# A three-layer transformer kernel with a rotation behind it: the set-up by first need, the skew product in it, and own tiles for attention's weights

## The chip, the cores and the metric

The kernel runs on one core of one Trainium2 chip. The metric is the device time of one execution in microseconds, as the median of several runs. The engines are TensorE (PE; its weight loads are PEld), VectorE (DVE), ScalarE (ACT), GpSimd (POOL) and SyncE (SP), which issues nearly all of the DMAs.

## What is computed

`x` is 32 sequences of 128 tokens with 144 channels, `cond` has one row of 144 for each sequence. Three transformer layers, modulated by `cond`, run one after another, and a rotation stands behind them. The first layer, in the reference's words:

```python
ada = jax.nn.silu(c) @ W_ada + b_ada
shift_msa, scale_msa, gate_msa, shift_mlp, scale_mlp, gate_mlp = jnp.split(ada, 6, axis=-1)
h = _modulate(_layernorm(x), shift_msa, scale_msa)
x = x + gate_msa * _attention(h, W_qkv, b_qkv, W_proj, b_proj)
h = _modulate(_layernorm(x), shift_mlp, scale_mlp)
mlp = jax.nn.gelu(h @ W_fc1 + b_fc1, approximate=True) @ W_fc2 + b_fc2
x = x + gate_mlp * mlp
```

Attention has 16 heads of 9 channels. The second layer's MLP is a mixture of four experts, of which each token takes two; the third layer has weights and biases on its layer norms. The last step:

```python
v = jax.nn.silu(cond) @ W.T + b                 # W: 2016 rows
A = A.at[:, iu, ju].set(v).at[:, ju, iu].set(-v)
R = expm(A)                                     # one 64 x 64 rotation for each sequence
U, _ = jnp.linalg.qr(P)                         # P: 144 x 64
z = jnp.einsum('btn,nd->btd', x, U)
z_rot = jnp.einsum('btd,bde->bte', z, R)
x_rot = x + jnp.einsum('btd,nd->btn', z_rot - z, U)
```

Everything is float32.

## The kernel before, in words

**Tiling.** All of x stays on the chip (tile `X`), tokens on partitions. The 144 channels of a contraction, with a row of ones for the bias, are 128 rows and 17 rows, so a weight matrix is loaded as a 128-row part and a 17-row part. The products of h with the weights are made of numbers in fp32r, as split products (`split_product`, L1000): the weights' rounded part (`Whi`), what it leaves (`Wlo`), and a third tile (`W3`) that stacks the 17 rows three times, against h in the same three forms (`hhi`, `hlo`, `h3`). One q/k product is 8 matmuls, shown as `L1000 x8`. The weights for both attention and MLP use the same three tiles, so each layer's weights are split twice on VectorE: `split` (L350 to L363) takes the 128-row part in two instructions and the 17-row part in pieces of 512 columns, through the tile `hshi`, which is h's too.

**Set-up.** SyncE loads, in this order: cond and constants, the layer-norm columns, the weights of the gates (`in_ada_gate`), x in four quarters, the weights of the columns (`in_ada_col`: shift and scale for three layers, twice, with the channels on partitions), the q/k/v weights of layer 0 (`in_wqkv`, 128 rows and three times 17), then the output weights `wp` of attention. TensorE transposes P for the QR decomposition, makes the gates (L978, L979) and then the columns, as 24 pairs of small products with the weights stationary (L989, L990). VectorE takes the statistics of the 32 sequences in a loop (L318) behind a wait for all of x, copies the gates, adds one to the scale columns on their way out of PSUM (L328), applies the third layer's layer-norm weights (L336, L342), splits the q/k/v weights, makes variance and inverse root of all sequences at once (`rstd_all`, L371 to L390), clears the tiles that attention needs clear (L427 to L432), and normalises the first pair (L396, L399). The gates are stored to memory and come back as one row for each sequence (`gate<-gates`, L246).

**Attention.** `pair(i)` for i from -2 to 17 runs two sequences in a pipeline of several stages on all engines: normalise, transpose (L1021), modulate on ScalarE (L809), four q/k products, each with a copy on ScalarE (L825) and a stacking step on VectorE (L446) that frees the one PSUM bank for the next; a v product, scores for the row maximum (L1057), the maximum (L458), scores again transposed (L1064), exponentials on ScalarE (L830), the product with v (L1079), the output product (L1111). pair(-2) and pair(-1) are the beginning of the pipeline only. The MLP runs in 8 groups of 4 sequences. During the last pair VectorE splits the MLP's weights, in the last MLP group the next layer's q/k/v weights (L350 and so on, called from `dense_step`), ahead of that group's last gated sums (L623) and statistics (L646).

**The tail.** Behind the last layer SyncE loads 17 rows of the skew weights (`in_skew_w`, 4096 columns; the 128-row part was loaded during the last layer), TensorE makes the 32 x 4096 skew product in eight banks (L1260, L1261), VectorE and ScalarE copy it out, SyncE stores it (`skew<-BIG`) and loads it back as 64 x 64 matrices (`BIG<-skew`), and the exponential of the matrices follows. The QR decomposition runs on GpSimd, in its own loop, with a broadcast through memory by GpSimd's queue in each step (`QB<-QA`).

The order of each engine's work is the order in which its program is written; engines meet by semaphores. SyncE's queue is one stream: a load behind a wait waits too.

## Time and profile before

| | us |
|---|---|
| median of 3 runs | 1677.52 (1673.40 to 1680.44) |
| profiled execution | 1683.87 |
| its span in the profile | 1682.1 |
| TensorE busy | 1447.5 (86%) |
| TensorE weight loads | 1187.5 (71%) |
| VectorE busy | 1022.9 (61%) |
| GpSimd busy | 830.7 (49%) |
| ScalarE busy | 750.1 (45%) |
| mean granted TensorE clock | 0.891 of full speed |

Busy shares are means over the whole span. The profile also gives, for any stretch of the span, a chain of waits: from its last instruction back to what released it, so that its pieces add up to the time that passed. A timeline lists each engine's instructions in order of time, with the idle time ahead of each in brackets and what ended it. The trace's times start with the span. PSA, PSB and PS are the PSUM tiles, without their numbers; BIG is one large tile that many stages share.

### The profile page before, as it was taken

Reading aid. Unit: us, or ns where it says so; the run is one execution under the profiler, and the core shown is the slowest. Engines: PE = TensorE matmul, PEld = TensorE weight load, DVE = VectorE, ACT = ScalarE, POOL = GpSimd, SP = SyncE. Lnnn points to the kernel's source line nnn. Section 1 sums busy time; section 2 is a strip of 40 time slices with the busy share of each in tenths; the row PEclk is TensorE's granted clock in tenths of the full one; section 3 lists DMA queues with packets and bytes.
Section 4 is the critical chain, followed back from the end, with each engine's and each line's share of the span. In section 5 each row is a group of like instructions: output and inputs, shape, how many; then the busy total and the mean of one; then the engine's idle time right before and its main releaser. Section 6 shows DMA issues by size and latency. Waiting matters only on the chain.

```text
span 1682.1 us, 39613 instructions
## 1 busy us (share of the span) xinstructions
PE 1447.5 (86%) x14380; PEld 1187.5 (71%) x14380; DVE 1022.9 (61%) x2471; ACT 750.1 (45%) x1484; POOL 830.7 (49%) x2444
## 2 busy tenths in 40 slices
PE   5499999679599999679999999679999949775599
PEld 3378888468488888469898999568888739705545
DVE  4589999645579999743333333459999845306511
ACT  0166666366266677343333332147767536300011
POOL 4666666666566566666667777777750000000000
PEclk9999999789689999879999999869999959956755
DMA  5211111312311211211112233333420021100001
GB/s 134 31 10 18 18 17 18 45 12 33 85 18 16 17 16 16 37 13 13 11 12 15 16 17 12 36 12 22 25 18 12 12 64 22 24 16 14 2 15 42
DMA packets 49363, 41.46 MB, mean 25 GB/s; under 512 B 8371, under 2 KB 45542, under 8 KB 48695
## 3 DMA queue, kind: packets, MB, share of 16 engines
q0 software_dynamic: 4224, 7.45, 12.4%
q1 hardware_dynamic: 44971, 31.79, 8.1%
q8 instruction: 104, 1.70, 0.4%
q14 instruction: 64, 0.52, 0.1%
HBM read 28.85 MB, written 2.99 MB: 19 GB/s over the span
## 4 chain that ended last, share of the span: by engine, by line
PE 82%; DVE 10%; ACT 3%; DMA 2%; issue 2%; SPq 1%; DVEq 0%; ACTq 0%
PE PS L1000 17%; PE PS L1211 14%; PE PSA L1000 12%; PE PSA L1057 6%; PE PS L1079 6%; PE PS L1093 3%; PE PS L1101 3%; PE PS L1214 2%; PE PS L1111 2%; DVE BIG L758 2%; PE PS L1112 1%; PE PSA L1269 1%; PE PS L1106 1%; PE PS L1329 1%; PE PS L1311 1%
## 5 line engine op out<-in xcount | busy, mean ns | idle before, releaser
L1211 PE MATMUL PS<-w,BIG 128*128 128x144 f32 (+1 forms) x1920 | 267.4, 287 | 4.7 <-DVE BIG L627 3.4
L1211 PEld LDWEIGHTS PS<-w,BIG 128*128 128x128 f32 (+1 forms) x1920 | 254.4, 191 | 12.8 <-DVE BIG L627 3.6
L909 ACT ACTIVATE BIG<-PSA 128x512 f32<-128x512 f32 (+1 forms) x224 | 131.6, 595 | 267.2 <-PE PSA L1000 267.1
L458 DVE TENSOR_REDUCE BIG<-PSA 128x8 f32<-128x1024 f32 x192 | 234.3, 1221 | 21.2 <-PE PSA L1057 17.2
L830 ACT ACTIVATE BIG<-PSB 128x1024 f32<-128x1024 f32 x192 | 196.8, 1025 | 105.6 <-PE PSB L1064 105.1
L825 ACT ACTIVATE qkhi<-PS 128x512 fp32r<-128x512 f32 x192 | 114.7, 597 | 101.8 <-PE PS L1000 95.1
L1000 PE MATMUL PS<-hhi,Whi 128*128 128x256 f32 x384 | 133.4, 347 | 21.8 <-DVE KK L446 10.1
L1057 PE MATMUL PSA<-KK,Q 32*128 32x128 f32 x1536 | 130.6, 288 | 4.7 <-DVE BIG L458 2.2
L1057 PEld LDWEIGHTS PSA<-KK,Q 32*128 32x128 f32 x1536 | 103.3, 190 | 39.5 <-issue 23.3
L1079 PE MATMUL PS<-BIG 128*32 128x128 f32 x3072 | 126.3, 283 | 4.1 <-ACT BIG L830 3.7
L1064 PE MATMUL PSB<-Q,KK 32*128 32x128 f32 x1536 | 127.9, 284 | 1.9 <-ACT BIG L830 1.9
L627 DVE SCALAR_TENSOR_TENSOR BIG<-PS,BIG 128x144 f32<-128x144 f32 x96 | 35.2, 368 | 151.4 <-PE PS L1214 151.4
L1377 POOL TENSOR_TENSOR qtree<-qtree 128x36 f32<-128x36 f32 (+3 forms) x384 | 101.6, 265 | 30.1
L1000 PE MATMUL PSA<-hhi,Whi 128*128 128x512 f32 (+1 forms) x224 | 102.4, 457 | 14.4 <-ACT BIG L909 8.8
L1000 PE MATMUL PS<-hhi,Wlo 128*128 128x256 f32 x384 | 113.2, 295 | 0.0
L1000 PE MATMUL PS<-hlo,Whi 128*128 128x256 f32 x384 | 112.8, 294 | 0.0
L1000 PE MATMUL PS<-h,W 128*128 128x256 f32 x384 | 112.4, 293 | 0.0
L1395 POOL MEMSET qprod<- 128x2 f32 x63 | 6.5, 103 | 208.6 <-DMA QB<-QA 208.6
L1000 PEld LDWEIGHTS PS<-hhi,Whi 128*128 128x128 f32 x384 | 76.6, 200 | 45.3 <-DVE KK L446 24.5
L1370 POOL DMA_DIRECT2D QB<-QA x128 | 81.9, 640 | 47.4 <-POOL QA L1410 18.9
L1064 PEld LDWEIGHTS PSB<-Q,KK 32*128 32x128 f32 x1536 | 100.9, 185 | 2.9 <-issue 2.5
L1382 POOL TENSOR_TENSOR qtree<-qtree 128x4 f32<-128x4 f32 (+3 forms) x384 | 83.1, 216 | 30.1
(272 smaller groups left out, 3877.1 us busy)
## 6 DMA issues: line engine op xcount, KB each, us to landing
gate<-gates SPq DMA_DIRECT2D x96, 72.0 KB, 2.9
mgate<-gates SPq DMA_DIRECT2D x96, 72.0 KB, 2.8
X<-in_x SPq DMA_DIRECT2D x4, 576.0 KB, 8.5
out<-X SPq DMA_DIRECT2D x8, 288.0 KB, 2.4
BIG<-in_skew_w SPq DMA_DIRECT2D x1, 2048.0 KB
BIG<-in_wqkv SPq DMA_DIRECT2D x3, 584.0 KB
w<-in_w SPq DMA_DIRECT2D x1, 1440.0 KB
BIG<-in_wm SPq DMA_DIRECT2D x1, 1154.0 KB
```

The lines of the kernel that those rows point to most:

```text
L458: V.tensor_reduce(nmax[:, :, 3 * HD + 2 * HP * a:3 * HD + 2 * HP * a + HP + 1:HP].rearrange("p g r -> p r g"), PSA[:, :].rearrange("p (r g ...
L825: S.activation(qkhi[:, :], PS[4][:, :], ACT.Copy).then_inc(qk_hi, 1)
L830: S.activation(PT[:, u % 2, a, :], PSB[:, :], ACT.Exp, scale=float(HD) ** -0.5).then_inc(exp_done, 1)
L909: S.activation(hm[0:rows, slot, :], PS[(par * FTOT[l] + j) % 2][0:rows, :], gelu).then_inc(gelu_done, 1)
L1000: last = mm(o, a, b, start=(k == 0), stop=(k == 3))
L1057: one = mm(PS[r][:, g * 128:(g + 1) * 128], Q[rows, par, g, q0:q0 + 128], KK[rows, par, g, q0:q0 + 128], start=True, stop=True)
L1064: two = mm(PS[2 + r][:, g * 128:(g + 1) * 128], KK[rows, par, g, q0:q0 + 128], Q[rows, par, g, q0:q0 + 128], start=True, stop=True)
L1079: last = mm(PS[6][p0:p0 + HP, at:at + 128], VA[:, u, G * g + 2 * a + r, :], PT[:, u % 2, a, (G * r + g) * 128:(G * r + g + 1) * 128], star ...
L1211: last = mm(o, hm[0:rows, slot, s * 128:(s + 1) * 128], w2[0:rows, FT * e + k, :], start=(k == 0), stop=(l != 1 and k == FT - 1))
L1370: pool.dma_start(QB[k % 2][:, k:C], row).then_inc(q_row[k % 2], 16)
L1377: link(R.tensor_tensor(t[:, 0:n, :], a[:, :, 0:half], a[:, :, half:2 * half], ALU.add))
L1382: link(R.tensor_tensor(t[:, 0:n, :], a[:, :, 0:half], a[:, :, half:2 * half], ALU.add))
```

## The change

In SyncE's program the loads come in another order: column weights of layer 0 by themselves, the first quarter of x, the q/k/v weights, the second quarter, the column weights of layers 1 and 2, the gates' weights, the last two quarters; then, behind the wait for the constants, the skew weights (in two halves of 2048 columns), `wp` and the layer-norm columns. The stores of the gates and of the skew product stand there too, ahead of the loads of the first MLP weights; after the last layer only the load of the matrices is left.

The columns are now products with silu(cond) stationary, 32 columns wide: four kinds of column lie on four strips of 32 in one bank (`column_products`), ScalarE adds one to the scales while it copies the bank, and TensorE transposes them (`columns_turn`). Gates and skew product use four strips in the same manner (`gate_products`, `skew_products`). Layer 0's columns are made first. Those of layers 1 and 2 and the gates are produced behind pair(-2) of layer 0, the skew product behind pair(-1), and `columns_rest` stands behind pair(0).

Statistics, variance and inverse root are functions of a range of sequences: the first 8 sequences are done ahead of pair(-2), the other 24 behind it, their inverse root behind pair(-1). `constant_parts`, the memsets of attention's tiles, stands behind pair(-2) in layer 0.

Attention's weights have tiles `Ahi`, `Alo`, `AW3` for themselves, those of the MLP `Mhi`, `Mlo`, `MW3`. The casts of attention's are ScalarE's (`qkv_cast`), and the 17-row part isn't cut into pieces of 512, for neither. In pair(-2) of layer 0 the q/k products use two banks in turn (`qk_bank`).

```diff
+        Ahi, Alo = sb("Ahi", [C0, WQKV], F32R), sb("Alo", [C0, WQKV], F32R)
+        AW3 = sb("AW3", [128, WQKV], F32R)
+        Mhi, Mlo = sb("Mhi", [C0, WMX], F32R), sb("Mlo", [C0, WMX], F32R)
+        MW3 = sb("MW3", [128, WMX], F32R)
...
+        def qk_bank(pn, j):
+            return PS[6 if pn == 0 and j % 2 else 4]
...
+            def load_ada(l, s):
+                sp.dma_start(AC0[l], d["ada_col"][0:C0, l * AC:(l + 1) * AC]).then_inc(s, 16)
+                sp.dma_start(AC1[l], d["ada_col"][C0:C + 1, l * AC:(l + 1) * AC]).then_inc(s, 16)
+            load_ada(0, ld_ada0)
+            def load_x(q):
                 sp.dma_start(X[:, q * 8 * C:(q + 1) * 8 * C].rearrange("p (b c) -> p b c", b=8),
...
+            load_x(0)
             load_raw("wqkv0", WQKV, ld_wq)
+            load_x(1)
+            load_ada(1, ld_ada)
+            load_ada(2, ld_ada)
+            sp.dma_start(AG0, d["ada_gate"][0:C0, :]).then_inc(ld_gw, 16)
+            sp.dma_start(AG1, d["ada_gate"][C0:C + 1, :]).then_inc(ld_gw, 16)
+            load_x(2)
+            load_x(3)
             sp.wait_ge(s_const, 1)
+            for h in range(2):
+                sp.dma_start(SW0[h], d["skew_w"][0:C0, h * SKH:(h + 1) * SKH]).then_inc(ld_skew, 16)
+                sp.dma_start(SW1[h], d["skew_w"][C0:C + 1, h * SKH:(h + 1) * SKH]).then_inc(ld_skew, 16)
...
+            sp.wait_ge(s_gev, 1)
+            for j in range(4):
+                sp.dma_start(gates_dram[:, j * GT:(j + 1) * GT], gate_rows[j * NB:(j + 1) * NB, :]).then_inc(s_gst, 16)
+            sp.wait_ge(sk_ev, 2)
+            for j in range(4):
+                sp.dma_start(skew_dram[:, j * 1024:(j + 1) * 1024], SV[j * NB:(j + 1) * NB, :]).then_inc(sk_st, 16)
+            sp.wait_ge(s_gst, 64)
+            sp.wait_ge(sk_st, 64)
             for l in range(LAYERS):
-                sp.wait_ge(s_split, SPLITS * (2 * l + 1))
+                sp.wait_ge(a_split, 2 * l + 2)
+                sp.wait_ge(s_cps, LAYERS)
                 load_raw(f"wm{l}", WM[l], ld_wm)
                 wait(sp, f2_done, n_unit(l) * MT)
+                sp.wait_ge(sk_ps, 2)
...
-            sp.dma_start(SW1, d["skew_w"][C0:C + 1, :]).then_inc(ld_skew, 16)
-            sp.wait_ge(sk_ev0, 4)
-            sp.wait_ge(sk_ev1, 4)
-            sp.dma_start(skew_dram, SV).then_inc(sk_st, 16)
-            sp.wait_ge(sk_st, 16)
...
+            def first_stats(q):
+                dve.wait_ge(ld_x[q], 16)
+                for b in range(8 * q, 8 * q + 8):
+                    V.bn_stats(st6[:, b:b + 1, :], xb(b)).then_inc(s_st0, 1)
+            def columns(l, ps):
+                dve.wait_ge(s_ct, 1 if l == 0 else LAYERS)
+                V.tensor_copy(col0[:, l, :, :], ps[:, 0:128].rearrange("p (k n) -> p k n", k=4))
+                V.tensor_copy(col1[:, l, :, :], ps[0:S3, 128:256].rearrange("p (k n) -> p k n", k=4)).then_inc(s_cev, 1)
...
+            def qkv_split(l):
+                wr, wr3 = raw(WQKV)
+                dve.wait_ge(a_cast, 2 * l + 2)
+                V.tensor_tensor(Alo[:, :], wr, Ahi[:, :].bitcast(F32), ALU.subtract).then_inc(a_split, 1)
+                V.scalar_tensor_tensor(AW3[0:S3, :], AW3[0:S3, :].bitcast(F32), K[0:S3, K_MW:K_MW + 1], wr3, ALU.mult, ALU.add)\
+                    .then_inc(a_split, 1)
+            def mlp_split(l):
+                n = WM[l]
+                wr, wr3 = raw(n)
+                dve.wait_ge(ld_wm, 64 * (l + 1))
+                V.tensor_copy(Mhi[:, 0:n], wr)
+                V.tensor_copy(MW3[0:S3, 0:n], wr3).then_inc(m_split, 2)
+                dve.wait_ge(m_split, 4 * l + 2)
+                V.tensor_tensor(Mlo[:, 0:n], wr, Mhi[:, 0:n].bitcast(F32), ALU.subtract)
+                V.scalar_tensor_tensor(MW3[0:S3, 0:n], MW3[0:S3, 0:n].bitcast(F32), K[0:S3, K_MW:K_MW + 1], wr3,
+                                       ALU.mult, ALU.add).then_inc(m_split, 2)
...
+                    first_stats(0)
+                    variance(0, 0, 0, 0, 8)
+                    columns(0, PS[1])
+                    inverse_root(0, 0, 0, 0, 8)
...
+                    if l == 0 and i == -2:
+                        qkv_split(0)
+                        for q in range(1, 4):
+                            first_stats(q)
+                        variance(0, 0, 1, 8, NB)
+                        dve.wait_ge(s_cps, LAYERS)
+                        dve.wait_ge(s_gps, 1)
+                        constant_parts()
+                    if l == 0 and i == -1:
+                        inverse_root(0, 0, 1, 8, NB)
+                    if l == 0 and i == 0:
+                        columns_rest()
...
+            def qkv_cast(l):
+                wr, wr3 = raw(WQKV)
+                act.wait_ge(ld_wq, 64 * (l + 1))
+                S.activation(Ahi[:, :], wr, ACT.Copy).then_inc(a_cast, 1)
+                S.activation(AW3[0:S3, :], wr3, ACT.Copy).then_inc(a_cast, 1)
+            def setup_rest():
+                column_rows(1, PS[2])
+                column_rows(2, PS[0])
+                act.wait_ge(s_gps, 1)
+                S.activation(gate_rows, PS[7][:, 0:GT], ACT.Copy).then_inc(s_gev, 1)
+            def skew_copies():
+                for h in range(2):
+                    act.wait_ge(sk_ps, h + 1)
+                    S.activation(SV[:, h * 512:(h + 1) * 512], PS[6 + h][:, :], ACT.Copy).then_inc(sk_ev, 1)
...
+                    if l == 0 and i == 0:
+                        skew_copies()
...
+                if l + 1 < LAYERS:
+                    qkv_cast(l + 1)
...
+            def column_products(l, ps):
+                for src, s, first in ((AC0, sc0, True), (AC1, sc1, False)):
+                    for kind in range(4):
+                        last = mm(ps[kind * NB:(kind + 1) * NB, 0:XW], s[:, :], src[l][:, kind * XW:(kind + 1) * XW],
+                                  start=first, stop=not first)
+                last.then_inc(s_cps, 1)
+            def columns_turn(l, ps):
+                pe.wait_ge(s_crow, l + 1)
+                nc.tensor.transpose(ps[:, 0:128], crow[:, l, 0:C0], ident)
+                nc.tensor.transpose(ps[0:S3, 128:256], crow[:, l, C0:XW], ident).then_inc(s_ct, 1)
+            def gate_products():
+                pe.wait_ge(ld_gw, 32)
+                for src, s, first in ((AG0, sc0, True), (AG1, sc1, False)):
+                    for j in range(4):
+                        last = mm(PS[7][j * NB:(j + 1) * NB, 0:GT], s[:, :], src[:, j * GT:(j + 1) * GT], start=first, stop=not first)
+                last.then_inc(s_gps, 1)
+            def skew_products():
+                pe.wait_ge(ld_skew, 64)
+                pe.wait_ge(s_gev, 1)
+                pe.wait_ge(qk_lo, 4)
+                for h in range(2):
+                    for src, s, first in ((SW0, sc0, True), (SW1, sc1, False)):
+                        for j in range(4):
+                            at = (j % 2) * 1024 + h * 512
+                            last = mm(PS[6 + h][j * NB:(j + 1) * NB, :], s[:, :], src[j // 2][:, at:at + 512], start=first, stop=not first)
+                    last.then_inc(sk_ps, 1)
+            pe.wait_ge(ld_cond, 48)
+            pe.wait_ge(s_silu, 4)
+            pe.wait_ge(ld_ada0, 32)
+            column_products(0, PS[0])
             pe.wait_ge(q_ld, 64)
             nc.tensor.transpose(PS[6][:, 0:C0], QP[:, 0, :], ident)
             nc.tensor.transpose(PS[6][:, C0:C], QP[0:C - C0, 1, :], ident[0:C - C0, 0:C - C0]).then_inc(q_ps, 1)
...
+            columns_turn(0, PS[1])
...
+                    wait(pe, qk_lo, n - 1 if n < 4 else n)
...
-                pe.wait_ge(va_set, 3 * (l + 1))
                 for i in range(-2, NB // 2 + 2):
+                    if i == 0:
+                        pe.wait_ge(va_set, 3 * (l + 1))
+                    if i == 1:
+                        pe.wait_ge(ld_wp, 160 * (l + 1))
                     pair(i)
...
+                    if l == 0 and i == -2:
+                        pe.wait_ge(ld_ada, 64)
+                        column_products(1, PS[2])
+                        pe.wait_ge(s_crow, 1)
+                        column_products(2, PS[0])
+                        gate_products()
+                    if l == 0 and i == -1:
+                        skew_products()
+                        pe.wait_ge(s_crow, LAYERS)
+                    if l == 0 and i == 0:
+                        pe.wait_ge(sk_ev, 2)
+                        columns_turn(1, PS[7][:, 0:256])
+                        columns_turn(2, PS[7][:, 256:512])
+                        pe.wait_ge(s_cev, LAYERS)
...
-            pe.wait_ge(ld_skew, 32)
-            for c in range(8):
-                mm(PS[c][0:NB, :], sc0[:, :], SW0[:, c * 512:(c + 1) * 512], start=True, stop=False)
-                mm(PS[c][0:NB, :], sc1[:, :], SW1[:, c * 512:(c + 1) * 512], start=False, stop=True).then_inc(sk_ps, 1)
```

SyncE, from the start of its queue, before:

```order
L204 DMA BIG<-in_ada_gate 128x864
L205 DMA BIG<-in_ada_gate 17x864
L207 DMA X<-in_x 128x8x144 x4
L210 DMA BIG<-in_ada_col 128x2148
L211 DMA BIG<-in_ada_col 17x2148
L215 DMA BIG<-in_wqkv 128x1168
L217 DMA BIG<-in_wqkv 17x1168 x3
L223 DMA wp<-in_wp 18x144 [waits constants_set]
```

The same engine after the change, from behind the column weights of layer 0:

```order
L227 DMA X<-in_x 128x8x144
L233 DMA BIG<-in_wqkv 128x1168
L235 DMA BIG<-in_wqkv 17x1168 x3
L227 DMA X<-in_x 128x8x144
L221 DMA BIG<-in_ada_col 128x716
L222 DMA BIG<-in_ada_col 17x716
L221 DMA BIG<-in_ada_col 128x716
L222 DMA BIG<-in_ada_col 17x716
L250 DMA mgate<-in_ada_gate 128x864
L251 DMA BIG<-in_ada_gate 17x864
L227 DMA X<-in_x 128x8x144 x2
L256 DMA BIG<-in_skew_w 128x2048 [waits constants_set]
```

Two of the four x loads and everything of the q/k/v weights are in front of the gates' weights; the last two quarters of x stand behind them, and the skew weights behind these.

VectorE, before, behind the third layer's column steps: the split of the q/k/v weights (the row L363 fills up the semaphore), and the first row of the variance (`mean`):

```order
L350 CAST Whi<-BIG 128x1168 [waits columns_product,constants_set,wqkv_loaded,columns_steps]
L352 TENSOR_TENSOR Wlo<-BIG,Whi 128x1168 [waits weights_split]
L356 CAST hshi<-BIG 51x512
L358 SCALAR_TENSOR_TENSOR W<-hshi,K,BIG 51x512 [waits weights_split]
L356 CAST hshi<-BIG 51x512 [waits weights_split]
L358 SCALAR_TENSOR_TENSOR W<-hshi,K,BIG 51x512 [waits weights_split]
L356 CAST hshi<-BIG 51x144 [waits weights_split]
L358 SCALAR_TENSOR_TENSOR W<-hshi,K,BIG 51x144 [waits weights_split]
L363 MEMSET epst 128x1 [waits weights_split]
L371 TENSOR_TENSOR mean<-st 128x32 [waits first_stats]
```

VectorE after the change, behind the second normalised sequence (the memsets and the step `hlo`, the low part of h, follow these rows):

```order
L384 TENSOR_TENSOR Alo<-BIG,Ahi 128x1168 [waits qkv_weights_cast]
L385 SCALAR_TENSOR_TENSOR AW<-AW,K,BIG 51x1168
L353 BN_STATS st<-X 128x6 [waits x_loaded1]
L353 BN_STATS st<-X 128x6 x7
L353 BN_STATS st<-X 128x6 [waits x_loaded2]
L353 BN_STATS st<-X 128x6 x7
L353 BN_STATS st<-X 128x6 [waits x_loaded3]
L353 BN_STATS st<-X 128x6 x7
L404 TENSOR_TENSOR mean<-st 128x24 [waits first_stats]
L405 TENSOR_TENSOR rtmp<-st 128x24
```

The split waits for casts of ScalarE and not for its own; three waits for quarters of x now lie between the split and `hlo`.

TensorE, before, from the end of the first pair's fourth q/k product through its v product (128x144) to its first scores (`PSA<-KK,Q`):

```order
L1000 MATMUL PS<-h,W 128x256
L1000 MATMUL PS<-Whi,hhi 128x144 [waits hf_ready]
L1000 MATMUL PS<-Wlo,hhi 128x144
L1000 MATMUL PS<-Whi,hlo 128x144
L1000 MATMUL PS<-W,h 128x144
L1000 MATMUL PS<-Whi,hhi 128x144
L1000 MATMUL PS<-Wlo,hhi 128x144
L1000 MATMUL PS<-Whi,hlo 128x144
L1000 MATMUL PS<-W,h 128x144
L1057 MATMUL PSA<-KK,Q 128x128 [waits qk_stacked]
L1057 MATMUL PSA<-KK,Q 128x128 x7
```

TensorE after the change, from the same q/k product to the v product (the scores follow behind it, as before):

```order
L1099 MATMUL PS<-hlo,Ahi 128x256
L1099 MATMUL PS<-h,AW 128x256
L1079 MATMUL PS<-BIG,sc 32x512 [waits qk_stacked,gates_copied,skew_loaded]
L1079 MATMUL PS<-BIG,sc 32x512 x3
L1079 MATMUL PS<-w,sc 32x512 x2
L1079 MATMUL PS<-BIG,sc 32x512 x6
L1079 MATMUL PS<-w,sc 32x512 x2
L1079 MATMUL PS<-BIG,sc 32x512 x2
L1099 MATMUL PS<-Ahi,hhi 128x144 [waits hf_ready,va_set,column_rows_ready]
L1099 MATMUL PS<-Alo,hhi 128x144
L1099 MATMUL PS<-Ahi,hlo 128x144
L1099 MATMUL PS<-AW,h 128x144
```

Sixteen skew matmuls of 32 rows by 512 columns, with three waits ahead of them, now stand between the fourth q/k product and the v product, which itself waits for rows of the other layers' columns.

## Rows read from the trace of the kernel before

**Rows 1.** Chain, the first 120 us: start us, length us, what.

```profile
13.73 11.86 DMA BIG<-in_ada_col
...
67.19 2.09 PE PS L1000 x8
```

**Rows 2.** Timeline of VectorE: start us, us, line, operation, out<-in, count.

```profile
47.61 0.73 DVE L336 SCALAR_TENSOR_TENSOR col<-col,lnc 128x32 f32<-128x32 f32 x4
```

**Rows 3.** Chain over the tail.

```profile
1465.91 12.51 DMA BIG<-in_skew_w
1478.55 1.88 PE PSA L1260 x2
...
1506.24 1.85 PE PS L1261 x2
1508.78 3.86 DMA skew<-BIG
1513.40 4.49 DMA BIG<-skew
1517.91 1.24 DVE BIG L720
```

**Rows 4.** Windows: PE, PEld, DVE, ACT, POOL, PE clock, DMA share, GB/s.

```profile
24.00:25.00 1.00, 0.00 (x0) 0.00 (x0) 0.64 (x3) 0.00 (x0) 0.00 (x0) 1.00 2.20 104
28.00:29.00 1.00, 1.00 (x7) 0.87 (x6) 0.62 (x2) 0.00 (x0) 0.97 (x3) 1.00 0.07 28
36.00:37.00 1.00, 1.00 (x6) 0.87 (x5) 0.00 (x0) 0.00 (x0) 0.67 (x2) 1.00 0.05 13
```

**Rows 5.** DMA issues: tiles, queue, count, KB each.

```profile
BIG<-in_wqkv SPq DMA_DIRECT2D x3, 77.6 KB
...
BIG<-in_skew_w SPq DMA_DIRECT2D x1, 272.0 KB
```

**Rows 6.** Timeline, TensorE and VectorE; brackets: idle before, what ended it.

```profile
10.46 1.62 PE L978 MATMUL PSA<-BIG,sc 128*32 128x432 f32 x2 [2.33 <-DMA BIG<-in_ada_gate]
...
17.80 0.31 DVE L318 BATCH_NORM_STATS2 st<-X  x1 [9.78 <-DMA X<-in_x]
```

**Rows 7.** Timeline of VectorE, before the first product and at a layer's end.

```profile
54.74 0.21 DVE L371 TENSOR_TENSOR mean<-st 128x32 f32<-128x32 f32 x1
...
58.45 0.48 DVE L427 MEMSET BIG<- 128x512 f32 x1 [0.17 <-DVE rstd L390]
...
61.73 0.34 DVE L396 TENSOR_SCALAR xh<-X,mean,rstd 128x128 f32<-128x128 f32 x1
...
438.35 0.93 DVE L646 BATCH_NORM_STATS2 st<-X 128x6 f32<-128x144 f32 x4
```

**Rows 8.** Timeline of TensorE, first scores.

```profile
81.44 1.11 PE L1057 MATMUL PSA<-KK,Q 32*128 32x128 f32 x8
```

**Rows 9.** Timeline of TensorE, a product on four strips.

```profile
315.93 1.08 PE L1079 MATMUL PS<-BIG 128*32 128x128 f32 x16
```

**Rows 10.** Timeline of VectorE, split at the end of layer 0.

```profile
431.33 0.78 DVE L350 CAST Whi<-BIG 128x1168 fp32r<-128x1168 f32 x1
432.14 1.39 DVE L352 TENSOR_TENSOR Wlo<-BIG,Whi 128x1168 fp32r<-128x1168 f32 x1
...
433.90 0.74 DVE L358 SCALAR_TENSOR_TENSOR W<-hshi,K,BIG 51x512 fp32r<-51x512 f32 x1
...
436.19 0.36 DVE L358 SCALAR_TENSOR_TENSOR W<-hshi,K,BIG 51x144 fp32r<-51x144 f32 x1
...
436.68 0.52 DVE L623 TENSOR_TENSOR BIG<-PS,mgate 128x144 f32<-128x144 f32 x2
```

**Rows 11.** Timeline of ScalarE.

```profile
99.69 1.03 ACT L830 ACTIVATE BIG<-PSB 128x1024 f32<-128x1024 f32 x1 [1.33 <-PE PSB L1064]
...
428.30 1.28 ACT L797 ACT_TABLE_LOAD   x1
```

**Rows 12.** Chain in the second pair, from 96 us.

```profile
106.19 1.14 PE PS L1000 x8
```

322 lines of the change are left out of this document (142 added, 180 removed).

## The prediction, made before the changed kernel ran

> **What bounds the kernel now.** I read four views: the chain of work over the first 120 us, the DMA traffic microsecond by microsecond, the timelines at the seams between stages, and the chain over the tail. [rows 1] is the chain of the start: it runs through the landing of the column weights (`in_ada_col`), the column products, the column steps on VectorE (done at 47.6 [rows 2]) and then split, statistics and memsets on VectorE, until the first q/k product starts at 67.19. Nothing of the attention runs before that. At the other end [rows 3] the chain waits 12.5 us for 17 rows of the skew weights, then computes the skew products for 29.5 us (1478.55 to 1508.1), stores them (3.9), loads them back and has the matrices at 1517.91. Between the two, TensorE is nearly always busy, except at five seams, at which VectorE does a weight split that TensorE waits for.
>
> **What a narrow load costs.** [rows 4] decides the start. From 26 to 36 us the DMA share is 0.06 to 0.07, which is one engine of sixteen, at 28 GB/s; at 36 it ends. What is queued last then are three 17-row copies of the q/k/v weights, 77.6 KB each [rows 5]: they run one after another, on one engine. The tail says the same: 272 KB in 17 rows [rows 5] take 12.5 us [rows 3], 26 KB/us behind some 2 us of latency. So I count KB on that one engine: a 128-row load leaves a sixteenth of its size there, a 17-row load all of it. Before: gates 27+57, x 144, columns 67+143, q/k/v 36+233. The landings fit: gates at 10.4, x at 17.8 [rows 6], columns 25.6 [rows 1], q/k/v at 36; that is 18 KB/us from 5 to 17.8, while all engines are busy, and 26 after it, stalls of about 1.2 us by the Householder broadcasts included (the microsecond from 24 in [rows 4]). The Trainium skill ("DMA: Bandwidth & Descriptors", "Why a DMA increments its semaphore by 16 and not by 1") says why: a load runs on the largest number up to 16 that divides its slowest dimension, so 17 rows run on one engine, and always the lowest-numbered. The trace agrees for the three copies; which engine it is, no row shows.
>
> **Part 1: set-up (gain 12.4 us).** The new order on that engine is: columns of layer 0 (22+48 KB), x0 36, q/k/v 269, x1 36, columns of layers 1 and 2 140, gates 84, x2 and x3 72, skew 400. By the rates above: x0 lands at 10, q/k/v at 21.5, x3 at 36.0 (332 KB at 23), the skew weights at 52.4. x3, which was there at 17.8, now comes 18 us later.
> VectorE: the first quarter's statistics, its root and two normalised batches are done by about 17. The split waits for ScalarE's casts, which wait for q/k/v: 21.5 + 2.3 + 2.8 = 26.6. Then it waits for x3 at 36.0, and behind that wait stand the statistics of the last quarter (8 at 0.23 [rows 7] = 1.9), the variance (a third of the 3.7 us from 54.74 to 58.45 [rows 7], 1.2), the memsets (58.45 to 61.8 [rows 7], 3.4) and the low part of h (0.8), which TensorE needs. First q/k product at 36.0 + 7.3 = 43.4 instead of 67.19: 23.8 us earlier. The products of layers 1 and 2 and the gates lie in TensorE's idle time before it.
> From there to the first scores took 14.25 us (67.19 to 81.44 [rows 1, 8]). Now the first four q/k products use two banks, so the next need not wait for copy and stack; at 2.09 us each, with the transposes between, they end after 9.9 us. ScalarE comes with 1.1 us of rows of the other layers ahead of its fourth copy; copy and stack (0.6 + 0.75) bring 55.9. Only then come the skew products (their weights at 52.4 are in time, by 3.5 us), with the v product (1.75) behind them, which before lay beside the stack. The skew products were 29.5 us for 16 matmuls in line [rows 3]; on four strips I take the factor of the one product that runs so: 16 passes of 128 columns in 1.08 us [rows 9] where a quarter of the 0.92 us of a 512-column pass is 0.23, so 3.7 in line, factor 3.5. That is 8.3 us at TensorE's lower level (1.2 GHz). The bounds are 7.4 (factor 4) and 4.2 (the higher level already). The Trainium skill ("TensorEngine Tiling (Array Packing)", "Theoretical Speedup") allows up to 4; by it the sum would be better by 0.9 us. First scores at 55.9 + 8.3 + 1.75 = 65.9, 15.5 us earlier than before.
> Then columns_rest sits between the first and the second pair: four transposes (0.6) and four copies (0.9), then eight small steps (4 in 0.73 [rows 2], so 1.4), all ahead of the max row for which the v product waits: 3.1 us with their waits. 15.5 - 3.1 = **12.4**. The bounds are 0 to 28, see the rivals.
> The stores of gates and skew rows and three loads are now ahead of the first gate row on SyncE. The copies are done at 65, two stores and their wait end near 70, the row lands at about 79 and is first read some 11 us into the second pair, near 95: nothing, by 16 us of cover.
>
> **Part 2: splits (gain 8.2 us).** At the end of a layer the split stood 5.35 us on VectorE (431.33 to 436.68 [rows 10]) ahead of the last two sums. Now the casts are ScalarE's: two of 1168 columns at about 1.15 (1.03 for 1024 [rows 11]), begun when its last gelu is done at 428.3 [rows 11], so ready at 430.6, ahead of VectorE at 431.3. There remain 1.39 and one multiply-add of 1168 columns, 1.43 by the slope from 0.36 (144 columns) to 0.74 (512) [rows 10]: 2.8 + gaps. Gain 2.5, and between layers 1 and 2, where the same stands in a row and ScalarE is idle even longer, 2.7. The three MLP splits lose pieces of 512: each saved piece is about 0.45 us of fixed cost and gaps, one in layers 0 and 2, four in layer 1: 2.7, rounded to 3 with the memset. The bound below is 0, if the out-copies of ScalarE are late instead. Own tiles for attention's weights take no wait away that ended last in any row; I give them nothing.
>
> **Part 3: the tail (gain 46.7 us).** The load, products, copies and store all go. From 1465.91, when the last statistics end, only the load back is left: 1512.66 to 1517.91 was 5.25 us, so the matrices are there at 1471.2 instead of 1517.9. 46.7, bounds 45 and 48: a load begun after a stretch of idle engines is priced by 3.9 to 5.3 in [rows 3]. TensorE is at its lower level both when it starts these matrices now and when it started them before, so I add nothing for it.
>
> **Sum.** 12.4 + 8.2 + 46.7 = 67.3. The profiled execution took 1683.9 and would give 1616.6; the median of the runs is 1677.5, so the forecast is **1610.2 us** (0.960 of before).
>
> **Rivals.**
> *A: the narrow loads are not in the way*, because other engines take them in turn and all ends by bytes. The Trainium skill's fit ("DMA: Bandwidth & Descriptors", "Anatomy of one DMA — SWDGE (gpsimd) path"), 2.0 us and 436 KB per microsecond, is of this kind. By rows: x3 would land as in [rows 6] after some 5 MB, at about 20; then the split and 24 statistics bound VectorE and the first product starts near 31. 12.4 us better than forecast: 1598. Against it stands [rows 4]. 15%.
> *B: the engine runs at 18 KB/us all the way*, as from 5 to 17.8. All through the skew weights 1,117 KB then land at 67, x3 at 44; TensorE waits in front of the skew products with all of attention behind it. 11 us worse: 1621. For it: more of the set-up now goes through with all engines busy, and a queue that is full holds SyncE back. 12%.
> *C: the strips stand in line* and the skew products take 29.5: 21 us worse, 1631. [rows 9] speaks against it. 4%.
> *D: slower than before.* One mechanism: TensorE stays at its lower level into layer 0's attention, since the thin skew products (the 29.5 us of them in [rows 3] never brought it up) and the wait after the first pair come where it used to rise. A q/k product costs 2.09 instead of 1.14 us [rows 1, 12]; a pair of batches, near 14 us at the higher level and full of TensorE work, then costs some 11 more. The 67 us are eaten after 6 pairs of 16; at 10 the kernel takes 1720. Before, the level rises within some 30 us of the first product. 2%.
>
> **How the numbers follow.** The forecast has 67%. The range takes in A and B and the bounds of the tail and splits, 1594 to 1625; outside lie C, D and the ends of the bounds. 0.5% is about what a measurement of this kernel can tell from no change; faster needs less than 1669, which all but D and accidents give: 0.96, same 0.02, slower 0.02.
>
> **What would show it.** First q/k product at 43 (31 for A, 52 for B), with VectorE's longest wait before it on x's last quarter; one engine's share of DMA through 50 us; skew products 8 us, not waiting for their weights; about 3 us of TensorE idle after the first pair; split rows of 2.8 us at both layer seams; the matrices 5.3 us behind the last statistics. I am wrong if the first product comes later than 52, or the skew weights do.

## The result, and the profile after

The changed kernel takes **1605.55 us** (median of 4 runs, 1603.45 to 1612.98) where the kernel before took 1676.84 in the same series: ratio 0.9553, 95% interval 0.9524 to 0.9582. A second series gave 0.9571 (0.9542 to 0.9601). Two executions of the kernel before, at 3418.6 and 7202.8 us in the series of `one_bank`, are slow ones and left out everywhere. The forecast was 1610.2, ratio 0.960. The profiled execution took 1603.45 us, its span is 1601.7, against 1683.87 and 1682.1 before.

The head of the page and its clock row (tenths of full speed, 40 slices):

```profile
PE 1395.5 (87%) x14346; PEld 1162.1 (73%) x14346; DVE 1005.9 (63%) x2430; ACT 756.5 (47%) x1493; POOL 825.9 (52%) x2444
...
PEclk9799999889789999869999999979999997986755
```

The chain of waits over the first 110 us of the changed kernel (start us, length us, what), the lines that answer to [rows 1, 8]:

```profile
9.53 8.04 SPq L222
...
20.47 13.25 DMA X<-in_x
33.74 3.46 DVE st L353 x16
...
42.56 3.79 PE PS L1099 x16
...
52.55 0.76 DVE Q L490
53.31 0.14 issue
53.45 7.52 PE PS L1079 x32
60.97 1.91 PE PS L1099 x8
62.88 1.04 PE PSA L1156 x6
```

The chain no longer runs through the column products, it runs through x, and the first q/k product starts at 42.56 instead of 67.19. Ahead of x it runs through SyncE: the issue of one 17-row load of column weights (L222) took 8.04 us, so that the last quarters of x were issued only at 20.47. At 53.45 stand the skew products. Windows of 2 us of the same kernel (the columns as in [rows 4]) show what x waits for:

```profile
14.00:16.00 2.00, 0.91 (x4) 0.69 (x4) 1.04 (x4) 0.00 (x0) 0.00 (x0) 1.00 0.08 30
16.00:18.00 2.00, 0.21 (x1) 0.00 (x0) 0.00 (x0) 0.00 (x0) 1.58 (x4) 1.00 0.06 26
26.00:28.00 2.00, 0.00 (x0) 0.00 (x0) 1.44 (x7) 0.00 (x0) 1.45 (x3) 1.00 0.06 25
```

A DMA share of 0.06 to 0.08 at 25 to 30 GB/s: one engine of sixteen, as in [rows 4], first during the 17-row copies of the q/k/v weights and again during the narrow part of the columns. VectorE's timeline says the same (the bracket: idle time before, and what ended it); its last three rows are the split at the end of layer 0 and the sums behind it, which answers to [rows 10]:

```profile
23.03 1.38 DVE L384 TENSOR_TENSOR Alo<-BIG,Ahi 128x1168 fp32r<-128x1168 f32 x1 [7.99 <-ACT AW L859]
24.32 1.43 DVE L385 SCALAR_TENSOR_TENSOR AW<-AW,K,BIG 51x1168 fp32r<-51x1168 f32 x1
...
33.74 3.45 DVE L353 BATCH_NORM_STATS2 st<-X 128x6 f32<-128x144 f32 x16 [6.30 <-DMA X<-in_x]
...
413.53 1.36 DVE L384 TENSOR_TENSOR Alo<-BIG,Ahi 128x1168 fp32r<-128x1168 f32 x1
414.81 1.60 DVE L385 SCALAR_TENSOR_TENSOR AW<-AW,K,BIG 51x1168 fp32r<-51x1168 f32 x1
416.34 0.51 DVE L675 TENSOR_TENSOR BIG<-PS,mgate 128x144 f32<-128x144 f32 x2
```

And the chain over the tail, which answers to [rows 3]: the load of the matrices follows the last statistics at once.

```profile
1431.08 0.94 DVE st L698 x4
1432.77 4.42 DMA BIG<-skew
1437.30 1.24 DVE BIG L769
```

Both kernels were profiled a second time (in `before_again` and `after_again`, below). The places where each stage starts or ends, in us from the span's start, read from the timelines (a stage's end is the first row of the next variance). The profile shows a granted clock of 1.00 until its first record of it, also from 42.6 to 46 us of the changed kernel, where matmuls of 256 columns take 0.41 us as at the lower level. So a first rise is read here from the record and from the lengths of matmuls, and the mean clock of a kernel that rises late is shown too high:

| | before | again | after | again | after less before, first pair |
|---|---|---|---|---|---|
| first q/k product | 67.2 | 66.6 | 42.6 | 42.7 | -24.6 |
| first scores | 81.4 | 80.8 | 62.8 | 62.9 | -18.6 |
| TensorE's granted clock first rises | 94.1 | 99.3 | 46.3 | 46.5 | |
| attention of layer 0 ends | 327.9 | 329.7 | 308.1 | 308.1 | -19.8 |
| MLP of layer 0 ends | 439.4 | 441.4 | 418.8 | 418.8 | -20.6 |
| attention of layer 1 ends | 714.9 | 713.9 | 693.8 | 697.0 | -21.1 |
| MLP of layer 1 ends | 1086.9 | 1087.1 | 1061.5 | 1064.5 | -25.4 |
| attention of layer 2 ends | 1357.4 | 1352.9 | 1323.6 | 1333.7 | -33.8 |
| last statistics done | 1465.9 | 1461.2 | 1432.0 | 1442.3 | -33.9 |
| matrices there | 1517.9 | 1513.5 | 1437.3 | 1447.5 | -80.6 |

### The profile page after: what moved, and what is told of

Read it like the earlier page. It is cut to its first block, busy times and chain, and to the rows that moved or that the text cites. A ratio compares the mean times of both kernels' runs of the same rounds, so it can differ in the third digit from the quotient of the medians.

```text
span 1601.7 us, 39391 instructions
## 1 busy us (share of the span) xinstructions
PE 1395.5 (87%) x14346; PEld 1162.1 (73%) x14346; DVE 1005.9 (63%) x2430; ACT 756.5 (47%) x1493; POOL 825.9 (52%) x2444
## 4 chain that ended last, share of the span: by engine, by line
PE 83%; DVE 9%; ACT 3%; issue 3%; SPq 1%; DMA 1%; ACTq 0%; DVEq 0%
PE PS L1099 17%; PE PS L1326 14%; PE PSA L1099 13%; PE PSA L1156 7%; PE PS L1178 7%; PE PS L1192 3%; PE PS L1200 3%; PE PS L1329 2%; PE PS L1210 2%; PE PS L1211 2%; DVE BIG L807 1%; PE PS L1205 1%; PE PSA L1379 1%; PE PS L1437 1%; PE PS L1419 1%
## 5 line engine op out<-in xcount | busy, mean ns | idle before, releaser
L1099 PE MATMUL PS<-hhi,Ahi 128*128 128x256 f32 x384 | 131.5, 343 | 23.8 <-DVE h L441 14.7
L1099 PE MATMUL PSA<-hhi,Mhi 128*128 128x512 f32 (+1 forms) x224 | 102.4, 457 | 14.7 <-ACT BIG L992 9.1
L1099 PE MATMUL PS<-h,AW 128*128 128x256 f32 x384 | 112.2, 292 | 0.0
L1099 PE MATMUL PS<-hlo,Ahi 128*128 128x256 f32 x384 | 111.2, 290 | 0.0
L1099 PE MATMUL PS<-hhi,Alo 128*128 128x256 f32 x384 | 111.2, 290 | 0.0
L1099 PEld LDWEIGHTS PS<-hhi,Ahi 128*128 128x128 f32 x384 | 75.8, 197 | 46.3 <-DVE KK L490 21.0
L1178 PEld LDWEIGHTS PS<-BIG 128*32 128x32 f32 x3072 | 73.2, 110 | 34.5 <-issue 22.9
## 6 DMA issues: line engine op xcount, KB each, us to landing
X<-in_x SPq DMA_DIRECT2D x4, 576.0 KB, 13.8
```

The lines of the kernel that those rows point to most:

```text
L1099: last = mm(o, a, b, start=(k == 0), stop=(k == 3))
L1178: last = mm(PS[6][p0:p0 + HP, at:at + 128], VA[:, u, G * g + 2 * a + r, :], PT[:, u % 2, a, (G * r + g) * 128:(G * r + g + 1) * 128], star ...
```

## The experiments

All ratios are to the kernel before, run on the same chip in the same series.

**The same kernels again.** Nothing is edited.

> The changed kernel itself once more, as the base for the others of this series. My theory of the 80 us between the two profiled executions is 73 us of changed work and some 7 us of which the profiled execution of before was itself longer than its median, so the ratio to before stays at 0.955 (0.952 to 0.958). The rival, that the gain ahead of the tail (33.9 us where I had forecast 20.6) is all the change's, wants 0.951 or less.

Measured: 1611.7 us against 1681.0, ratio 0.9571 (0.9542 to 0.9601). No boundary up to 418.8 differs by more than 0.1 us from the first profiled execution, then layer 1's attention takes 278.2 us instead of 275.0 and layer 2's 269.2 instead of 262.1. The runs of this one kernel lie at 1602.6 with a mean granted clock of 0.905 and at 1616.2 with 0.894; over all runs of the study a line with one slope for all kernels gives 8.5 us (standard error 0.5) for 0.01 of mean clock.

> The kernel before, once more, for a second profiled execution of it. Attention of layer 2 with its seam to the MLP took 8.4 us more in the first profiled execution of before than in that of the changed kernel, where the prediction has 0.5. If that is the granted clock of one execution, the stretch from the first q/k product of layer 2 (1099.1) to its first MLP product (1374.7), 275.6 us, differs by 3 us or more this time, and the time at the boundaries of layer 0 stays within 1 us. If it is the change's, it is 275 to 276 again.

Measured: ratio 0.9991 (0.9963 to 1.0018). From the first q/k product of layer 2 to its first MLP product the execution took 271.0 us (1099.2 to 1370.2), 4.5 less than the first one; layer 0's boundaries differ by 2, more than I had said. So of the 8.4 us that layer 2's attention seems to gain (270.5 to 262.1 in the table), 4.7 go when one execution of before is put for the other, and 7.1 when one of after is. Over this stage the four executions had a granted clock of 0.91 (270.5 us, before), 0.92 (269.2, after again), 0.94 (265.8, before again) and 0.96 (262.1, after): the time goes by the clock and not by the kernel.

**Narrow loads.** Each 17-row load of the set-up in two:

```diff
+            def narrow(dst, src, s):
+                sp.dma_start(dst[0:16, :], src[0:16, :]).then_inc(s, 16)
+                sp.dma_start(dst[16:17, :], src[16:17, :]).then_inc(s, 16)
```

> One thing is changed: each 17-row load of the set-up is issued as 16 rows and 1 row. If a 17-row load runs on one engine and x's third and fourth quarter stood behind 332 KB on it, they land near 17 instead of 33.7, the statistics of three quarters and the memsets follow the split in a row, and the first q/k product starts at 29 (28 to 32) instead of 42.6: 11 to 13 us faster than the changed kernel. If all engines share the bytes anyway (rival A of the prediction), the first product stays at 42 to 43 and the time at that of the changed kernel, or 1 to 2 us above it for the nine further loads that SyncE issues.

Measured: 1598.5 us, ratio 0.9509 (0.9485 to 0.9533), by the medians 13.2 us less than `after_again` in the same series, by the two ratios 10.4, and 12.8 (standard error 1.2) at equal clock. Its chain:

```profile
11.52 9.45 DMA X<-in_x
20.99 3.46 DVE st L360 x16
...
29.78 3.79 PE PS L1106 x16
```

The first q/k product starts at 29.8 instead of 42.6. Same bytes, the same order, no other edit: the place behind narrow loads was the price. SyncE isn't held at a narrow load any more either (none takes over 0.7 us to issue), and it issues the last quarters of x at 11.52. The profiled execution doesn't show all of the gain at once: first scores come 13.8 us earlier (49.0), but attention of layer 0 ends 5.4 us earlier (302.7), with a granted clock of 0.92 over that stretch where the changed kernel had 0.97.

**VectorE's work moved behind.** Statistics, variance and memsets for the later sequences go from behind pair(-2) to behind pair(-1):

```diff
                     if l == 0 and i == -2:
                         qkv_split(0)
+                    if l == 0 and i == -1:
+                        dve.wait_ge(s_cps, LAYERS)
+                        dve.wait_ge(s_gps, 1)
+                        constant_parts()
                         for q in range(1, 4):
                             first_stats(q)
                         variance(0, 0, 1, 8, NB)
```

> The loads stay as in the changed kernel. VectorE's statistics of the last 24 sequences, their variance and attention's memsets are moved from between the split and the low part of h to behind pair(-1) of layer 0, where VectorE is idle for the 7.5 us of the skew products; ScalarE's root for them goes behind its copies of columns and gates. If x's late landing was what held the first q/k product, the next limit is TensorE's own program, where the gates' weights land at about 32 and the gate products end at 34: first q/k product at 34 to 35, 8 us earlier, and the moved work costs 1 to 2 us later, so 6 to 7 us faster than the changed kernel. If the late quarters were not the limit, nothing is gained (0 to 1).

> Both edits of the two runs before together. q/k/v weights land near 10, ScalarE's casts are done at 15.1, the split at 18, and columns and gates lie beside it: first q/k product at 19 to 21 instead of 42.6. The skew weights are all there by some 25, ahead of their products. 20 to 22 us faster than the changed kernel, near 1584. If single engines are not the limit, it does as late_stats does, 6 to 7 us.

Measured: 1610.4 us, ratio 0.9564 (0.9537 to 0.9590), and for both edits 1600.3 us, 0.9523 (0.9494 to 0.9551). The first q/k product came at 33.8 and at 22.4, nearly as expected. Both times were missed: `late_stats` takes what the changed kernel takes, `wide_and_late` what `wide_rows` takes. The chain of `wide_and_late`:

```profile
26.81 0.75 DVE KK L497
...
30.61 1.76 DVE BIG L477
...
32.71 4.91 DVE st L360 x23
...
39.61 0.76 DVE Q L497
40.37 0.14 issue
40.50 7.53 PE PS L1085 x32
```

The fourth stack (`Q L497`) of the first pair is the first thing that pair(0) does, and "behind pair(-1)" is ahead of it: 10 us of moved work stand between third and fourth stack, and the skew products wait for the fourth. I had looked for idle time of the engine and not for the row that is next in its program.

```diff
                     if at(-1):
                         h_second(i + 1, (i + 1) % 2)
+                    if l == 0 and i == 0:
...
+                        constant_parts()
+                        for q in range(1, 4):
+                            first_stats(q)
+                        variance(0, 0, 1, 8, NB)
+                        inverse_root(0, 0, 1, 8, NB)
```

> As wide_and_late, but the moved statistics, variance, inverse root and memsets stand on VectorE behind the fourth stack of the first pair (in pair(0), behind the low part of h), and ScalarE's root behind the skew copies. In wide_and_late and late_stats they stood ahead of that fourth stack, for which the skew products wait; VectorE needed 10 us there, and the first scores were no earlier. If that place is what ate the gain, the first q/k product stays at 22.4, the skew products start at 32 to 33 instead of 40.5 and the first scores at 42 to 44 (62.8 in the changed kernel): 7 us faster than wide_and_late's own first scores, and 4 to 6 us faster than wide_rows in the end, near 1593. If the time goes by TensorE's granted clock instead (it falls within 20 us of the first product, and in wide_rows attention of layer 0 took 8.4 us longer from its first scores than in the changed kernel), the end is no earlier than wide_rows'.

Measured: 1593.3 us, ratio 0.9471 (0.9448 to 0.9493), by the ratios 6.4 us less than `wide_rows` of the series before; the two intervals just meet. First scores at 40.4 instead of 49.9 (42 to 44 expected), the statistics now beside the skew products. As expected, the place had eaten it.

**The skew product.**

```diff
-                    for src, s, first in ((SW0, sc0, True), (SW1, sc1, False)):
-                        for j in range(4):
-                            at = (j % 2) * 1024 + h * 512
-                            last = mm(PS[6 + h][j * NB:(j + 1) * NB, :], s[:, :], src[j // 2][:, at:at + 512], start=first, stop=not first)
-                    last.then_inc(sk_ps, 1)
+                    mm(PS[6 + h][0:NB, 0:16], sc0[:, :], SW0[0][:, 0:16], start=True, stop=True).then_inc(sk_ps, 1)
```

> The changed kernel with the skew products left out (one product of 16 columns for each bank stands in their place, and ScalarE copies a constant instead; the rotation's matrices are then those of a constant): load, stores and all waits stay. The prediction says that the skew product costs 8.3 us where it stands and nothing elsewhere: first scores 7 to 7.5 us earlier (55.5), and the kernel 7 to 8 us faster than the changed one. If the thin products (32 rows of four strips) are also what pulls the granted clock down behind them (53 to 70 us in the changed kernel), the level stays up there and the gain is 12 to 15 us.

Here the rotation is made of a constant, which ScalarE copies in the product's place. Measured: 1602.6 us, ratio 0.9520 (0.9492 to 0.9548), by the two ratios of the changed kernel 5.5 to 8.5 us less. First scores at 55.8 instead of 62.8, and attention of layer 0 ends at 301.2 instead of 308.1: the 7 us are still there. The granted clock in windows of 2 us, the third column from the end:

```profile
50.00:52.00 2.00, 0.72 (x7) 0.52 (x5) 0.77 (x4) 2.00 (x7) 1.53 (x6) 1.00 0.05 13
52.00:54.00 2.00, 0.38 (x5) 0.37 (x5) 1.27 (x3) 1.32 (x5) 1.81 (x6) 0.77 0.14 32
54.00:56.00 2.00, 2.00 (x10) 1.87 (x12) 0.20 (x1) 1.07 (x2) 1.64 (x4) 0.50 0.19 43
```

It falls at 53 as with the skew products, so they are not what pulls it down, and the rival is refuted. It comes back at 63.4 instead of 70.2, earlier by what the products took. What stands before the fall in both is TensorE waiting from 50.4 for the fourth stack; that this wait is the cause is not shown.

> The skew product is back behind the last layer, with its load of 17 rows, its copies and its store there, but on four strips; everything else is as in the changed kernel. The prediction's parts: in the tail 12.5 us for the narrow load, 8.3 (7.5 by the trace of the changed kernel) for the products, some 1.2 for the last copy, 3.9 for the store and 0.6 between them, 25 to 26 us, less the 7.5 us that the set-up is rid of: 17 to 19 us slower than the changed kernel, ratio to before 0.967. Of the tail's 46.7 us the strips are then 22, the place 25. If the products in the set-up had been hidden, the whole 25 to 26 us are lost.

The edit is the changed kernel's `skew_products`, called where the product stood before. Measured: 1624.7 us, ratio 0.9681 (0.9648 to 0.9714), by the ratios 18.5 to 21.5 us more than the changed kernel. The tail from last statistics to matrices takes 29.9 us (12.4 narrow load, 7.6 products, 2.2 store, 4.5 load back, the rest copies and issue): 22.1 less than before, 24.6 more than in the changed kernel. So of the tail's 46.7 us strips, shorter copy and store are 22 and the place 25. In the set-up the first scores come 9.1 us earlier (53.7), of which the profiled execution shows only 0.5 at the end of layer 0's attention (307.6), again with a granted clock of 0.92 in between.

**The casts.** In layers 1 and 2 they go back to VectorE, and ScalarE's are taken out:

```diff
+                if l:
+                    V.tensor_copy(Ahi[:, :], wr).then_inc(a_cast, 1)
+                    V.tensor_copy(AW3[0:S3, :], wr3).then_inc(a_cast, 1)
```

> In layers 1 and 2 VectorE makes the casts of attention's weights itself again (0.8 and 0.8 us, as whole instructions of 1168 columns), own tiles and ScalarE's casts in layer 0 stay. The prediction gives the casts on ScalarE at each of the two seams 1.6 of the 2.5 to 2.7 us: 3 us slower than the changed kernel. By the two profiled executions the first of these seams gave 0.8 us only, with its split off the chain; then it is 1 to 1.5 us slower in all, inside the noise.

Measured: 1621.6 us, ratio 0.9641 (0.9618 to 0.9663). By the timelines the seams (end of the MLP's last product with its first weights to the start of the next layer's first q/k product) take 22.4 and 30.6 us, in the changed kernel 20.9 and 28.8: 3.3 us in all, as expected. By the medians it is 10 or more, by the two ratios 12 to 15, but these runs had a mean clock of 0.8925 against 0.902, and at equal clock 4.4 (standard error 1.2) are left. Why this kernel drew the lower clock in five of six runs, I can't say.

**Two banks, and the clock.** `qk_bank` gives PS4 always, each product waits for the stack before it:

> The changed kernel with the first pair's four q/k products on one bank again, each waiting for the stack of the one before. By the rows of before they then take from the first product to the fourth stack 4.3 us more than the 10 us of the changed kernel, so first scores at 67 instead of 62.8. The skew weights are there by 53 and hide nothing of it. 4 us slower than the changed kernel; with the mean granted clock of the runs a scatter of 5 us lies over it, so I read it from the first scores and from the times at equal clock. If ScalarE's rows for the other layers' columns were the limit anyway, it is 1 us.

Measured: 1614.2 us, ratio 0.9587 (0.9560 to 0.9614), by the two ratios 3 to 6 us more than the changed kernel. First scores at 66.7, 3.9 later. But attention of layer 0 ends at 316.2, 8.1 later, more than the ratios leave at the end. The other 4.2 are the clock: between first scores and that end TensorE stood at its lower level until 79.1 and from 85.9 to 92.7, in the changed kernel until 70.2 and from 80.4 to 87.2. Two rows of TensorE's timeline of each kernel, first `after`, then `one_bank` (a product of 256 columns takes 0.41 at 1.2 GHz, 0.28 at 2.4):

```profile
46.14 0.43 PE L1099 MATMUL PS<-hhi,Ahi 128*128 128x256 f32 x1
46.52 0.27 PE L1099 MATMUL PS<-hlo,Ahi 128*128 128x256 f32 x1
```

```profile
77.79 0.41 PE L1099 MATMUL PS<-h,AW 128*128 128x256 f32 x1
...
80.52 0.28 PE L1099 MATMUL PS<-hlo,Ahi 128*128 128x256 f32 x1
```

With two banks the higher level comes 3.7 us after the first product, with one 36 us after it. The one difference on TensorE up to there is the waiting, 1.5 us behind each of the first two products and 0.6 behind the third.

> The kernel before with one thing of the change: the first pair's q/k products use two banks in turn, here in all three layers. My theory: what they give is the wait for each stack (4.3 us in each first pair) and, behind it, the earlier rise of TensorE's granted clock. With one bank it rose 27 to 33 us after the first q/k product of layer 0 (before, 94.1 against 67.2; one_bank, 79.1 against 42.9, though it was set up as the changed kernel is), with two banks 4 us after it (46.3 against 42.6). So here it should rise within 6 us of the first product, near 71 to 73, fall once more behind the wait for the first stack of the second half, and each layer's stretch from the first to the last q/k product shrink by 4 to 9 us: 18 us faster than before in all, ratio 0.989 (0.986 to 0.993). The rival, that the early start of the changed kernel or its lighter work on GpSimd and the DMA queues let the level rise, leaves it at 94: then 3 x 4.3, 13 us, ratio 0.992 or more, and no rise before 90 in the trace.

Measured: 1667.1 us, ratio 0.9902 (0.9881 to 0.9923). In the kernel before, with this edit alone:

```profile
72.72 0.41 PE L1003 MATMUL PS<-h,W 128*128 128x256 f32 x1
...
74.33 0.28 PE L1003 MATMUL PS<-hhi,Wlo 128*128 128x256 f32 x1
```

It rises at 73.2, 5.7 us after its first product, 21 us earlier than in before. The ratio alone doesn't decide, for its interval takes in the 0.992 of the waits; the trace does. The rival, that the lighter set-up let the level rise, is out for this kernel. From the first q/k product to the end of layer 0's attention the execution took 254.1 us instead of 260.7, 4.5 of it ahead of the first scores. Attention of layers 1 and 2 (273.0 and 265.5 us, in the two executions of before 275.5 and 272.6, 270.5 and 265.8) shows nothing clear of the clock's scatter.

**Put together.** `wide_and_late2`, with two banks and late memsets (behind the low part of h) at the start of every layer, the columns of layers 1 and 2 turned ahead of the skew products, and their layer-norm columns loaded earlier:

```diff
-            return PS[6 if pn == 0 and j % 2 else 4]
+            return PS[6 if pn % (NB // 2) == 0 and j % 2 else 4]
...
+                    if i == -1:
...
+                        constant_parts()
```

> wide_and_late2, and what the changed kernel does for layer 0 done for layers 1 and 2 too: the first pair of each layer on two banks (4.3 us each), attention's memsets behind the low part of h of the first pair, where VectorE waits for the first q/k product, and not ahead of the first normalised rows (3.4 us each, of which some 0.6 comes back ahead of the first stack, so 2.8). In layer 0 the columns of layers 1 and 2 are turned and finished ahead of and beside the skew products, not behind the first pair (2.4 us of idle TensorE there). 2 x 7.1 + 2.4, some 16 us less than wide_and_late2: ratio to before 0.937, near 1577. The stretch from the last product of the MLP to the first q/k product should be 18 instead of 21 us before layer 1. If the granted clock falls further where less waiting is left, half of it is lost.

Measured: **1571.9 us, ratio 0.9333 (0.9309 to 0.9357)**, 6.7% less than before and 2.3 to 2.5% less than the changed kernel. It is 5 us better than expected, and I can't say from which of its edits. Its chain at layer 1's start:

```profile
395.47 4.13 issue
399.60 0.45 PE PS L1121
...
403.43 0.39 DVE h L448
...
405.27 1.76 DVE BIG L476
...
407.15 0.76 DVE KK L493
```

The seam, read as for the casts, is 386.6 to 403.9: 17.3 us, 20.9 in the changed kernel. The memsets now stand ahead of the first stack, and no longer ahead of the normalised rows. In layer 0 the first scores are later than in `wide_and_late2` (45.0 against 40.4), but its attention ends 8.3 us earlier (285.6 against 293.9).

## Why the prediction was right, step by step

**What bounds, and the narrow load.** Right in what ends last. The wait for x's late quarters (6.3 us) is the last long one of VectorE before the first product; it is not its longest, as I had it, for the one for the q/k/v casts is 8.0. The rest was near: q/k/v weights were cast from 20.8 (I had 21.5), x0's statistics ran from 9.7 (10), the first q/k product started at 42.56 (43.4). That it came so near is in part luck: x landed at 33.7 and not at 36.0, but behind it stood the statistics of two quarters (3.46 us) where I had counted one (1.9), and 8.8 us passed to the product instead of 7.3. `wide_rows` turns the argument into a test. That test also shows that rival A, the narrow loads out of the way, had the right price (12.4, measured 10 to 13) for a thing that this kernel doesn't do. B wanted the first product behind a landing at 44: refuted. In the sentence on the Trainium skill ("DMA: Bandwidth & Descriptors", "Why a DMA increments its semaphore by 16 and not by 1") the rule of the slowest dimension is borne out: 16 rows and 1 row instead of 17, nothing else.

**The first pair and the skew product.** First scores at 62.8 where I had 65.9. The row of products and stacks ended at 53.3 (55.9 forecast): 0.8 us of that is the earlier start, the rest is that I priced all four products at the lower level and two ran at the higher. The skew products were 7.5 us (8.3; the bound of factor 4 was 7.4): 29.5 by 7.5 is 3.9. The rule of the Trainium skill ("TensorEngine Tiling (Array Packing)", "Theoretical Speedup"), up to 4, was nearer here than my row of another product with its 3.5. Rival C is refuted.

**columns_rest.** 3.1 forecast; TensorE sat idle for 0.97 and 1.42 us there, 2.4, and did four transposes.

**The step that fell short: the clock in part 1.** The sum let the rest of attention in layer 0 stand as before plus 3.1 us: 249.6 from the first scores on. `one_bank` took 249.5, the changed kernel 245.3. The two banks not only shortened the first row, they brought the higher level 33 us earlier (46.3 against 79.1), and that gave 4.2 us which no term had. I had the clock as a rival for the worse only (D), and its mechanism does show in small: the level fell at 53.1 until 70.2 and at 80.4 until 87.2, each time behind a wait. But with the rise at 46.3 in place of 94.1 the balance was a gain. Part 1 was 12.4 by forecast and is 19.8 at the end of layer 0's attention (its MLP split, 1.2, included). No run takes back the order of the loads, the products with silu(cond) stationary or the divided statistics one by one, so how the 24.6 us at the first product divide among them is argued from the chain and not shown.

**Part 2.** The splits of q/k/v gave 2.8 and 4.9 us at the seams (2.5 and 2.7 forecast). The seams before were 427.7 to 451.4 and 1065.4 to 1099.1, after 409.9 to 430.8 and 1044.7 to 1073.5. At the second, ten passes of TensorE behind the wait for the split also took 1.49 us this time and not 2.77, the level having stayed up. In the table the first seam's 2.8 leave only 0.8 (this MLP stage took 110.7 us instead of 111.5), since its part ahead of the seam took 101.8 instead of 99.8, with a granted clock of 0.88 instead of 0.89; more of its cause I don't know. The MLP splits are 2.3, 7.9 and 2.3 us instead of 3.5, 9.6 and 2.9: 3.5 us for the 3 forecast, read as lengths on VectorE; no run takes them back, and attention of layer 1, where the longest stands, took 275.0 us against 275.5. 11.2 against 8.2 by these rows. `casts_on_vector` confirms the casts' 1.6 us each.

**Part 3.** 46.7 forecast. From the last statistics to the matrices: 52.0 before, 5.3 after, 46.7.

**The sum** was 67.3 against 71.3 by the medians. By the two profiled executions it is 80.4, of which that of before lay 7 us above its median and that of after 2 below; by the second two it is 66.6. So the total was met nearer than its parts: the start and the splits gave more than forecast, and the scatter by the clock, 8 to 9 us for 0.01, is larger than what is left.

## What to carry to other kernels

Weights with an odd number of rows beside 128 are cheap in bytes and dear in the queue: look for a DMA share of one engine, and split the load so that its rows divide, as 17 rows into 16 and 1 here. What is "behind" a loop iteration in the code may be ahead of the last step of a pipeline: read the engine's own rows before work is moved into its idle time. And remove small waits between the first dense products of a stage first, since here they also held the clock down for the work behind them.

## What the runs showed of the hardware

- Waits of 1.5 us behind the first two products, of 2.1 us each, held TensorE at its lower level for 27 to 36 us (three executions); without them it rose 3.7 us after the first product in the changed kernel and 5.7 us after it in the kernel before.
- Once up, it fell to 0.5 again: in the changed kernel behind 3 us with TensorE idle (50.4 to 53.5), for 17 us with the skew products and for 10 without them; in `before_two_banks` at 80.1 for 3.4 us, with no wait longer than 0.75 us ahead of it. What makes it fall is open.
- Executions of one kernel differ in their mean granted clock by 0.01, and in their time by 8 to 9 us with it. A gain of 5 us is to be read from one place in the trace and not from the medians.
- A load of 17 rows went at 25 to 30 KB/us, and SyncE was held for 8.0 us at the issue of one of them. Issued as 16 rows and 1 row, neither shows: the DMA share is above 1.0 from 10 to 22 us, and x's last quarters landed at 21.0 and not at 33.7.
